# A gated cross-attention and FFN kernel: batch 0's scores one slot earlier, the first masks loaded by ScalarE's queue at the start, and a reordered second stage

## What is computed

```python
def _L0_xattn_ref(hidden_states, memory_tokens, memory_mask):
    scores = jnp.einsum('bsd,bmd->bsm', hidden_states, memory_tokens) * scale
    scores = jnp.where(memory_mask[:, None, :], scores, neg_inf)
    attn = jax.nn.softmax(scores, axis=-1)
    readout = jnp.einsum('bsm,bmd->bsd', attn, memory_tokens)
    ...
def _L0_ffn_ref(x, w_gate, w_up, w_down):
    h = jax.nn.silu(x @ w_gate) * (x @ w_up)
    h_sparse = _sparsify_2to4(h)          # the 2 largest |h| of every 4
    return h_sparse @ w_down
x = x + jnp.tanh(g_xattn[0]) * _L0_xattn_ref(_layernorm(x), ctx_2048, mask)
x = x + jnp.tanh(g_ffn[0]) * _L0_ffn_ref(_layernorm(x), w_gate, w_up, w_down)
```

## Time and profile before

| | us |
|---|---|
| median of three runs | 1080.91 |
| profiled execution | 1081.23 |
| its span | 1079.4 |
| TensorE busy | 1069.8 |
| VectorE busy | 795.1 |
| ScalarE busy | 611.6 |
| GpSimd busy | 225.8 |

### The profile page before, as it was taken

One profiled execution on the slowest core, in us unless ns is written; L12 is line 12 of the kernel. 1 busy time (PEld: TensorE's weight loads), 2 busy tenths in 40 slices (PEclk: granted clock), 3 DMA queues, 4 the chain that ended last, 5 costly groups with the idle time before them and its releaser, 6 DMA issues.

```text
span 1079.4 us, 15220 instructions
## 1 busy us (share of the span) xinstructions
PE 1069.8 (99%) x5000; PEld 881.5 (82%) x5000; DVE 795.1 (74%) x1389; ACT 611.6 (57%) x1126; POOL 225.8 (21%) x343
## 2 busy tenths in 40 slices
PE   8999999999999999999999999999999999999998
PEld 7888877888888888888888888888888888888887
DVE  6999889998987676677757576676866464665756
ACT  7999786777755454444544454444544444443452
POOL 6888411211111111110001111111000111111121
PEclk9999999999999999999999999999999999999999
DMA  9998986999899777888799777888797667676726
GB/s 315 319 315 292 384 332 151 341 315 303 269 280 363 169 198 185 217 233 240 204 298 281 185 182 205 202 222 243 202 331 221 155 154 189 153 191 152 205 25 144
DMA packets 89822, 252.67 MB, mean 234 GB/s; under 512 B 9104, under 2 KB 9872, under 8 KB 85648
## 3 DMA queue, kind: packets, MB, share of 16 engines
q1 hardware_dynamic: 68144, 203.45, 54.1%
q0 software_dynamic: 21600, 48.24, 26.6%
HBM read 153.09 MB, written 98.57 MB: 233 GB/s over the span
## 4 chain that ended last, share of the span: by engine, by line
PE 92%; DMA 2%; DVE 2%; issue 2%; ACT 1%; SPq 0%; POOL 0%; ACTq 0%; DVEq 0%; POOLq 0%
PE ps_y L1431 11%; PE ps_y L1429 11%; PE ps_y L1430 11%; PE ps_a L1335 10%; PE ps_a L1333 10%; PE ps_a L1337 10%; PE ps_d L1333 5%; PE ps_d L1337 5%; PE ps_d L1335 5%; PE ps_y L1397 3%; PE ps_c L1360 2%; PE ps_c L1337 2%; PE ps_c L1335 2%; PE ps_c L1333 2%; PE ps_a L1352 1%
## 5 line engine op out<-in xcount | busy, mean ns | idle before, releaser
L634 POOL DMA_DIRECT2D out_rows<-y_out x124 | 105.6, 852 | 705.9 <-ACT y_out L786 702.9
L786 ACT ACTIVATE y_out<-ps_y,ffn_gate 128x512 f32<-128x512 f32 x124 | 85.4, 689 | 241.2 <-PE ps_y L1431 241.2
L1333 PE MATMUL ps_a<-xm,w_ring 128*128 128x512 f32 x512 | 199.8, 390 | 0.5 <-DVE hidden L1056 0.5
L1335 PE MATMUL ps_a<-xm,w_ring 128*128 128x512 f32 x512 | 199.6, 390 | 0.0
L1337 PE MATMUL ps_a<-xm,w_ring 128*128 128x512 f32 x512 | 199.5, 390 | 0.0
L1431 PE MATMUL ps_y<-dn,h_lo 128*128 128x512 f32 x480 | 187.2, 390 | 0.0
L1429 PE MATMUL ps_y<-dn,h_hi 128*128 128x512 f32 x480 | 187.1, 390 | 0.0
L1430 PE MATMUL ps_y<-dn,h_hi 128*128 128x512 f32 x480 | 186.7, 389 | 0.0
L1070 DVE TENSOR_TENSOR beats<-h_abs 128x512 bf16<-128x512 f32 x186 | 117.8, 686 | 1.3 <-ACT h_abs L756 1.3
L1333 PEld LDWEIGHTS ps_a<-xm,w_ring 128*128 128x128 f32 x512 | 96.1, 188 | 21.4 <-issue 1.0
L1337 PEld LDWEIGHTS ps_a<-xm,w_ring 128*128 128x128 f32 x512 | 96.1, 188 | 20.2
(11 more groups left out here) (124 smaller groups left out, 1875.6 us busy)
## 6 DMA issues: line engine op xcount, KB each, us to landing
w_ring<-w_scratch SPq DMA_DIRECT2D x147, 512.0 KB, 4.4
out_rows<-y_out POOLq DMA_DIRECT2D x124, 256.0 KB, 4.1
w_scratch<-w_ring SPq DMA_DIRECT2D x56, 512.0 KB, 6.6
xm_scratch<-x_out SPq DMA_DIRECT2D x40, 512.0 KB, 5.8
xm<-xm_scratch SPq DMA_DIRECT2D x19, 1024.0 KB, 10.0
w_raw<-in_L_ffn_w_down SPq DMA_DIRECT2D x9, 1024.0 KB, 7.4
x_in<-in_x SPq DMA_DIRECT2D x32, 256.0 KB, 4.9
ctx_in<-in_ctx SPq DMA_DIRECT2D x32, 256.0 KB, 5.2
```

Of the source, the lines that this page charges most:

```text
L634: nc.gpsimd.dma_start(out[RING * (n // (2 * TILES * QS)) + TILES * ORDER[order] + n % TILES], y_out[:, n % 4], accum_op=ALU.add).then_inc( ...
L786: nc.scalar.activation(y_out[:, n % 4], ps_y[n % 2][:], ACT.Identity, scale=ffn_gate[:]).then_inc(y_copied, 1)
L1333: nc.tensor.matmul(to, w_ring[:, k, e, 0, c], xm[:, k, 0, c], start=begins and c == 0, stop=False, skip_group_check=not begins)
L1335: nc.tensor.matmul(to, w_ring[:, k, e, 0, c], xm[:, k, 1, c], start=False, stop=False, skip_group_check=not begins)
```

## The change

On the start: the six idle transposes behind `score(0)` are gone; the mask of batches 0 to 7 is loaded by ScalarE's queue as its very first instruction instead of by SP behind the loads of batch 2, and converted by GpSimd ahead of the first mean instead of in slot 1; VectorE masks batch 0's scores in slot 2 instead of slot 3. In the second stage: in steps 0 and 1 VectorE's order puts batches of comparisons, `keep` and `h_low` further ahead and `w_low`(2, 6), `add_c11`(2) and the split of x(1, 0, 1) further back; ScalarE's `copy_d0`(2) comes after two `h_high` instead of four; in steps 6, 10 and 14 `copy_d0` and `add_c22` come ahead of the x split.

```diff
-CONVERT = {1: 0, 3: 1, 4: 2, 21: 3}
+CONVERT = {3: 1, 4: 2, 21: 3}
...
-IDLE_TURNS = (12, 10, 6)
+IDLE_TURNS = (12, 10)
...
             for b in range(INPUTS):
                 load(b)
-                if b == 2:
-                    load_mask(0)
...
+            convert(0)
             for n in range(-1, SLOTS - 1):
...
+            nc.scalar.dma_start(mask_in[:, 0:GROUP_M], mask.rearrange("b m -> (b m)")[0:GROUP_M]
+                                .rearrange("(a n) -> a n", a=1).to_broadcast([P, GROUP_M])).then_inc(mask_loaded[0], 16)
             for n in range(SLOTS):
...
                     if s == 1:
                         copy_a1(u, 0)
                         copy_a1(u, 1)
-                        for j in tiles:
+                        for j in tiles[:2]:
                             h_high(0, 0, j)
                         copy_d0(u, 0)
                         copy_d0(u, 1)
+                        for j in tiles[2:]:
+                            h_high(0, 0, j)
...
-                        x_high_at(s, 0)
+
+                        if s < QS or s % QS != 2:
+                            x_high_at(s, 0)
                         copy_d0(u, 0)
                         copy_d0(u, 1)
+                        if s > QS and s % QS == 2:
+                            x_high_at(s, 0)
...
-                b = n - 3
-                if 0 <= b < B:
+
+                b = 0 if n == 2 else n - 3
+                if 0 <= b < B and n != 3:
...
-                    if s > QS:
+                    if s > QS and s % QS != 2:
                         x_low_at(s, 0)
                     add_c22(u, 0)
                     add_c22(u, 1)
+                    if s > QS and s % QS == 2:
+                        x_low_at(s, 0)
...
                 elif s == 1:
-                    w_low(dve, nc.vector, 2, 6)
-                    add_c11(2, 0)
-                    add_c11(2, 1)
+
                     for j in tiles[:2]:
                         h_low(0, 0, j)
+                    keep(0, 0, tiles[2:])
+                    w_low(dve, nc.vector, 2, 6)
                     add_c22(u, 0)
                     add_c22(u, 1)
                     for j in tiles[2:]:
                         h_low(0, 0, j)
+                    add_c11(2, 0)
+                    add_c11(2, 1)
+                    x_low_at(0, 1)
                     compare(0, 1, first + second)
...
                     w_sum(dve, 2, 2)
+                    gated0(1, 0)
                     w_sum(dve, 2, 3)
-                    gated0(1, 0)
                     gated0(1, 1)
...
                     w_low(dve, nc.vector, 2, 3)
-                    x_low_at(0, 1)
+                    compare(0, 0, REST + second)
                     w_low(dve, nc.vector, 2, 4)
+                    count_wins(0, 0)
                     w_low(dve, nc.vector, 2, 5)
-                    compare(0, 0, REST + second)
-                    count_wins(0, 0)
-                    keep(0, 0, kept_order(0))
+                    keep(0, 0, kept_order(0)[:2])
                     continue
...
             score(0)
-            idle_turns(IDLE_TURNS[2])
             turn_x(1)
```

More of the change, by code:

```diff
@@ L580, in _, with convert @@
             pool.wait_ge(half_done, 1)
+            def convert(m):
+                pool.wait_ge(mask_loaded[m], 16)
+                part_m = slice(m * GROUP_M, (m + 1) * GROUP_M)
+                nc.gpsimd.tensor_scalar(mask_neg[:, part_m], mask_in[:, part_m], -BIG, BIG, ALU.mult,
+                                        ALU.add).then_inc(mask_neg_done, 1)
+            convert(0)
             for n in range(-1, SLOTS - 1):
@@ L604, in _ @@
                 if n in CONVERT:
-                    m = CONVERT[n]
-                    pool.wait_ge(mask_loaded[m], 16)
-                    part_m = slice(m * GROUP_M, (m + 1) * GROUP_M)
-                    nc.gpsimd.tensor_scalar(mask_neg[:, part_m], mask_in[:, part_m], -BIG, BIG, ALU.mult,
-                                            ALU.add).then_inc(mask_neg_done, 1)
+                    convert(CONVERT[n])
                 for u, blk in SPREAD_AT.get(n, ()):
```

## The result

| | before | after |
|---|---|---|
| median of ten runs, us | 1081.20 (1080.05 to 1082.78) | 1084.59 (1083.65 to 1085.57) |
| ratio, 95% interval | | 1.0025 (1.0017 to 1.0033) |
| profiled execution, us | 1081.23 | 1084.64 |
| its span, us | 1079.4 | 1082.6 |

What follows compares the result with a forecast made beforehand. TensorE was taken to set the end, with VectorE as full from 149.4 to 182.4 us. Gains of 0.45 + 0.37 + 0.52 = 1.3 us gave a median of 1079.6 us, range 1078.3 to 1081.5.

Steps and rivals of the forecast that it cites:

- Part 1, x(0) beside the mask: Start: the mask's 128 KB beside x(0) delay it by 0.35 us, 0.45 by the DMA rate, 1 us as bound.
- part 1: All start edits together: 0.45 us gained, between -0.2 and +0.7.
- Part 1, the conversion ahead of the mean: Start, GpSimd: the mask, in at about 3.4 us, is converted by 4.5, so converting before mean(0) costs nothing.
- Rival (b): Start: late mask landing holds the first mean 3 us; 1082.3 us in all, chance 0.08; sign: GpSimd idle beyond 4.5 us.
- Part 1, the removed turns and the earlier scores: Start: without six idle transposes and with earlier scores, TensorE's work after 13.89 us comes up to 0.7 us earlier.
- Rival (c): Start: the removed transposes were needed to keep TensorE's clock up; 2.4 us lost, 1082.0 us, chance 0.02.
- Part 2, the give-back: Second stage: of 2.8 us gained by 168, TensorE loses some 2.4 us in new waits near 182 and 197.
- Rival (a): Second stage: the gap closed at 167 us is kept whole; 3.8 us gained in all, 1077.1 us, chance 0.05.
- Part 2, the gain: Steps 0 and 1 of the second stage: 0.37 us kept past 197.33 us, bounds 0 and 0.5.
- Cost nothing: Second stage: the later x split and the stores of w_ring(2) behind it still end before ScalarE needs them.
- Part 3: Steps 6, 10, 14: step 6's 0.52 us wait goes, bounds 0.3 and 0.52; nothing in steps 10 and 14.
- The sum: Whole kernel: 0.45 + 0.37 + 0.52 = 1.3 us gained, median 1079.6 us; chance 0.77.

Runs made afterwards that it cites:

- mask_behind_x0: unmoved_d0 with the first mask's load issued by ScalarE only once x(0) has landed; 1079.39 us, 0.9984 of the kernel before.
- mask_act_rows: Kernel before, ScalarE's first instruction loading 128 different 1 KB rows of x(31) in place of the first mask; 1081.5 us against 1081.86, one run.
- mask_act_only: Kernel before with only the first mask's load moved to ScalarE's queue as its first instruction; 1085.60 us against 1081.86.
- start_only: Kernel before with only the change's start edits (early mask load and conversion, idle transposes gone, earlier scores); 1084.05 us against 1081.82.
- unmoved_d0: mask_unmoved_w25 with ScalarE's copy_d0 of unit 3 ahead of its x split in step 1; 1079.45 us against 1081.87.
- mask_unmoved_w25: Changed kernel with the mask's load and conversion back in place and w_low(2,5) ahead of count_wins(0,0); 1080.44 us against 1081.86.
- mask_unmoved_no01: Kernel before without the six idle transposes, with batch 0's scores earlier and the new x order in steps 6, 10, 14; 1081.16 us against 1081.87.
- mask_act_two: mask_act_only with the mask of batches 8 to 15 loaded by ScalarE's queue right behind the first; 1083.7 us against 1081.87, one run.
- mask_act_bcast_x: Kernel before, ScalarE's first instruction broadcasting one 1 KB row of x(31) to 128 partitions in place of the first mask; 1084.23 us against 1081.86, one run.
- after_w25: Changed kernel with VectorE's w_low(2,5) put back ahead of count_wins(0,0); 1083.32 us against 1081.82 for the kernel before.

## Why the prediction was wrong, point by point

**Part 1, x(0) beside the mask: the step that failed.** "At 289 GB/s, the rate of the fourth microsecond, that is 0.45 us more before x(0) is in", 0.35 taken, 1 us as the bound. Measured 2.78 us, which alone turns the forecast gain of part 1 into a loss. The arithmetic of bytes was right for a load of bytes: 0.55 us with 128 different rows. The mistake was to price the transfer by its size and to overlook its shape, one row for 128 partitions, although the trace had a row on it: its own masks took 5.3 us at least to land, and in its eighth microsecond the rate was 152 GB/s. The prediction saw the first and put it down to the full queue, where x loads took 5.4 us as well. The rule of the Trainium skill that was weighed ("DMA: Bandwidth & Descriptors", section "Issuing engines are not separate DMA queues") has the right sign, and mask_behind_x0 agrees with it, in that the issuer did not matter; by bytes alone it gives the prediction's 0.45 us, near the 0.55 us of mask_act_rows and far from 2.78.

**Part 1, the conversion ahead of the mean.** "So the conversion itself costs nothing" rested on a mask landing ahead of x(0). It landed at 6.49 and the conversion held the mean back by 0.3 us. Rival (b) has the mask landing at "6.0 to 6.5" and the mean three microseconds late, which is what came about (7.61 against 4.50), but with another cause for nine tenths of it: (b) has x(0) in at 2.6 us and the mean waiting for the mask, where in fact x(0) was late itself, and mask_act_only loses as much without the conversion in front. So (b)'s 0.08 was too little, and its sign (GpSimd idle for `mask_in` beyond 4.5 us, here until 6.49) came for another reason. Its 1082.3 us also fell short of 1084.6.

**Part 1, the removed turns and the earlier scores.** Up to 0.7 us was forecast with nothing else late; with the mask unmoved the first `probs` is turned at 13.52, 13.51 and 13.11 against 13.89: 0.4 to 0.8. What spreads them is a thing that the prediction read wrongly, TensorE's clock at the start. It took the 1.00 of the earlier trace rows for the clock from 0 to 14 us. But the traces' records of the granted clock begin only some microseconds into the execution, and where there is no record the rows read 1.00. In all fifteen traces the first record is one of full clock. In the thirteen in which TensorE is at work at that moment its pace changes just there, from one transpose every 0.21 us to one every 0.11. The ten idle turns behind the first ctx show it:

```profile
5.02 1.25 PE L1367 MATMUL ps_y<-ident 128*128 128x128 f32 x10
```

```
kernel               first clock record, us    the ten turns, us
mask_behind_x0        4.59                     1.25
before                4.75                     1.25
start_only            4.85                     1.26
unmoved_d0            6.28                     1.84
mask_unmoved_w25      7.30                     2.34
mask_unmoved_no01     7.30                     2.33
after                12.40                     2.34
mask_act_only        12.65                     2.34
```

Every kernel makes its first twelve turns at the slow pace (2.82 us for twelve). mask_act_two has records that go down as well: full clock from 4.42, half from 7.84 to 11.25, full again, and its turns take the slow pace within that stretch, one every 0.21 us:

```profile
8.00:9.00 1.00, 1.00 (x6) 1.00 (x6) 0.88 (x2) 0.65 (x1) 0.25 (x3) 0.50 1.06 406
```

So the slow pace of the other kernels ahead of their first record is that of the lower level, 1.2 GHz. That is read from the pace; no record covers it.

In the eight kernels whose first ctx is in by 4.6 us the clock rises between 4.59 and 7.30 us. Of the seven that wait for it until 6.4 to 7.2 us, five rise only between 9.70 and 12.65; start_only had risen ahead of the wait and kept its clock; mask_act_two had risen too and fell behind it. From the mean of x(0) to the first `probs` the changed kernel needs 9.33 us, start_only with the same start 8.46. So the gain of the turns and the earlier scores was there (0.93 us against the 9.39 before), and the clock took back 0.87 of it. That the late rise follows from the wait is likely by the count of the kernels, and start_only shows that it needn't.

Rival (c) had this in view, the low clock in the first 14 us, at a chance of 0.02 and a price of 2.4 us, and its sign, a granted clock under 1.00 before 14 us, can't be read from the rows for want of records. Its cause was another: it looked for it in the missing turns, but mask_act_only and mask_act_bcast_x have all their turns and rise as late (12.65 and 12.57), and the third bunch of turns, at 13.15 in mask_act_only, comes behind the rise, as it does in every kernel that has it.

**Part 2, the give-back.** Right in its places and in its size: waits near 182 and 197, "together some 2.4 us", came as 1.61 + 0.54 + 0.27 = 2.4 us. Rival (a) is out.

**Part 2, the gain.** 0.37 us was forecast, and the changed kernel lost 0.35 there. The step that failed is "Cost nothing" under "What else moves": it followed the x split and the stores, but not `w_low`(2, 5), which the edit moved behind `count_wins`, and for which ScalarE waits. after_w25 takes out 1.3 us by this alone. With it mended part 2 is worth 169.61 - 168.65 = 0.96 us in the profiles of kernels that start early, and 169.35 - 168.66 = 0.69 in those that start late (mask_act_only and mask_act_bcast_x beside after_w25), beyond the bound of 0.5 either way: VectorE's full row behind 169 held less back than "0.4 us earlier" said. What the gap at 167 costs through the clock behind it, about 1.4 us in about half of the runs, stands in none of the prediction's terms.

**Part 3.** The wait went, as forecast. Its size was that of one execution: the 0.52 us are right for the earlier trace rows, counted from start to start, but other executions lost from next to nothing to 1.79 us there. The medians give 0.24 us with an interval that holds 0 and 0.52, so its worth is open.

**The sum.** With the mask left where it was and `w_low`(2, 5) mended the measured gain is 1.4 us, the sum was 1.3. That is partly luck, since part 2 was worth more and part 3 less, and since part of it is the price of the clock behind the gap: against the runs of the kernel before at 1.000, with a median of 1080.90 in that session, mask_unmoved_w25 gains 0.5 us and not 1.4. (Its one profiled execution, at 1.000 like that of the kernel before, has a span 1.5 us shorter; the runs can't say more closely how much is luck.) The changed kernel, added up from its landmarks: + 3.05 at the start, + 0.35 to unit 3, - 0.2 behind it, 3.2 us.

## What to carry to other kernels

Price a DMA by what it reads, not only by its bytes: in these traces one row broadcast to all partitions in the first microseconds about halved the rate of everything beside it, and it belongs behind the load that heads the critical chain. When operations are moved past each other on a full engine, list for each of them who waits for its semaphore, also across two units and on another engine: here the one that was overlooked cost 1.3 us, more than the reordering brought. An early gain must pass every later wait whose time is fixed by something else, so read the next such wait before counting it. And where a view reads a full clock, check it against the pace of the instructions.

## What the runs showed of the hardware

- A load of 1 KB of one row into 128 partitions, issued 0.7 us into the execution: the DMA rate from 2 to 5 us was 66 to 200 GB/s in six kernels, against 251 to 396 with 128 different rows; x(0) was used at 5.8 to 6.3 us instead of 3.4 to 4.0. Behind a load of other rows it slowed the others all the same (142 and 143 GB/s); a second broadcast right behind it did not (370 and 409). The cause is open.
- Behind one and the same gap of 2.3 to 2.45 us TensorE's granted clock fell to half for 3.4 us in three profiles of nine, whatever the gap's exact length, at a price of about 1.4 us; the mean clock of the runs points to about half of all executions (45 of 85).
- At the start TensorE ran its transposes at half pace (one every 0.21 us instead of 0.11) until 4.6 us in one kernel's execution and until 12.7 in another's. The first record of its granted clock begins at the change of pace; the 1.00 that the rows read ahead of it stands for no record.
